# Turning softmax probabilities in one DVE instruction with a DMA block exchange, and reordered opening and seam work

## The reference

```python
xn = _layernorm(x); h = rmsnorm(xn) * ln_weight
h_q, h_k, h_v = h @ w_q.T, ctx @ w_k.T, ctx @ w_v.T       # (8, 128, 32 heads, 128)
score = einsum('bqhd,bkhd->bhqk', h_q, h_k) + position_bias
score = softmax(where(mask, score, -inf)); score = where(mask, score, 0)
out = einsum('bhqk,bkhd->bqhd', score, h_v).reshape(8, 128, 4096) @ w_out.T
x = x + tanh(g_xattn) * (xn + out)
x = x + tanh(g_ffn) * (base(x') + top-2 of 28 rank-8 experts(x')),  x' = _layernorm(x)
```

## Time and profile before

| | us |
|---|---|
| median of three runs | 888.44 (887.14 to 889.11) |
| the profiled execution | 888.88 |
| its span | 887.1 |
| PE busy in it | 867.6 |
| DVE / ACT / POOL busy | 655.4 / 359.6 / 308.5 |
| one iteration of the main loop | 40.47 |

### The profile page before, as it was taken

One profiled execution on the slowest core, in us unless ns is written; L12 is line 12 of the kernel. 1 busy time (PEld: TensorE's weight loads), 2 busy tenths in 40 slices (PEclk: granted clock), 3 DMA queues, 4 the chain that ended last, 5 costly groups with the idle time before them and its releaser, 6 DMA issues.

```text
span 887.1 us, 15278 instructions
## 1 busy us (share of the span) xinstructions
PE 867.6 (98%) x5128; PEld 768.2 (87%) x5128; DVE 655.4 (74%) x1295; ACT 359.6 (41%) x966; POOL 308.5 (35%) x218
## 2 busy tenths in 40 slices
PE   8989999998999999999999999999999999999998
PEld 7868888887998989898999989898989999898786
DVE  6885655659696877778696968778686969698863
ACT  5564444444253353434252443434252524444320
POOL 1476656686132332423142323323231423222200
PEclk9999999999999999999999999999999999999999
DMA  9124454454121221212121211203121202211001
GB/s 317 39 95 154 152 190 154 156 175 143 48 100 48 76 87 37 100 34 91 47 85 39 100 60 64 95 30 100 47 77 47 100 26 98 93 52 55 18 25 71
DMA packets 29074, 78.23 MB, mean 88 GB/s; under 512 B 4352, under 2 KB 6400, under 8 KB 27136
## 3 DMA queue, kind: packets, MB, share of 16 engines
q1 hardware_dynamic: 29056, 78.00, 25.6%
HBM read 60.16 MB, written 17.83 MB: 88 GB/s over the span
## 4 chain that ended last, share of the span: by engine, by line
PE 85%; DVE 8%; POOL 2%; issue 2%; DMA 1%; ACT 1%; SPq 0%; POOLq 0%; DVEq 0%; ACTq 0%
PE proj_ps L1112 53%; PE proj_ps L1285 13%; PE score_ps L1143 3%; PE score_ps L1171 3%; PE proj_ps L1463 2%; DVE attn L909 2%; PE pv_ps L1171 2%; PE turn_ps L1171 2%; PE proj_ps L1229 1%; PE pv_ps L1143 1%; PE turn_ps L1143 1%; PE proj_ps L1481 1%; DMA w_raw<-in_weights 1%; PE pv_ps L1112 1%; PE turn_ps L1112 1%
## 5 line engine op out<-in xcount | busy, mean ns | idle before, releaser
L347 POOL TENSOR_TENSOR w_lo<-w_raw,w_hi 128x1024 fp32r<-128x1024 f32 x49 | 118.4, 2417 | 360.9 <-ACT w_hi L444 287.0
L909 DVE STREAM_TRANSPOSE attn<-attn 32x256 f32<-32x256 f32 x480 | 209.1, 436 | 6.7
L1112 PE MATMUL proj_ps<-w_hi,ct_hi 128*128 128x256 f32 x512 | 146.2, 285 | 0.0
L1112 PE MATMUL proj_ps<-w_lo,ct_hi 128*128 128x256 f32 x512 | 144.8, 283 | 0.0
L1112 PE MATMUL proj_ps<-w_hi,ct_lo 128*128 128x256 f32 x512 | 144.8, 283 | 0.0
L925 DVE TENSOR_TENSOR acc<-proj_ps,acc 128x512 f32<-128x512 f32 x112 | 77.5, 692 | 66.7 <-PE proj_ps L1112 65.8
L464 ACT ACTIVATE attn<-attn,neg_max 128x128 f32<-128x128 f32 x256 | 99.2, 389 | 36.4 <-DVE neg_max L890 36.4
L444 ACT ACTIVATE w_hi<-w_raw 128x1024 fp32r<-128x1024 f32 x49 | 51.9, 1058 | 122.7 <-PE proj_ps L1112 118.8
L1112 PEld LDWEIGHTS proj_ps<-w_hi,ct_lo 128*128 128x128 f32 x512 | 98.2, 192 | 0.7
L1112 PEld LDWEIGHTS proj_ps<-w_hi,ct_hi 128*128 128x128 f32 x512 | 98.2, 192 | 0.7
L1112 PEld LDWEIGHTS proj_ps<-w_lo,ct_hi 128*128 128x128 f32 x512 | 98.1, 192 | 0.0
(11 more groups left out here) (199 smaller groups left out, 1777.6 us busy)
## 6 DMA issues: line engine op xcount, KB each, us to landing
w_raw<-in_weights SPq DMA_DIRECT2D x67, 512.0 KB, 3.3
q_spill<-attn SPq DMA_DIRECT2D x60, 256.0 KB, 3.0
qt<-q_spill SPq DMA_DIRECT2D x15, 1024.0 KB, 7.3
acc<-in_x SPq DMA_DIRECT2D x4, 512.0 KB, 8.9
bias_sb<-in_bias SPq DMA_DIRECT2D x16, 128.0 KB, 2.0
out<-attn SPq DMA_DIRECT2D x8, 256.0 KB, 2.0
w_raw<-in_x SPq DMA_DIRECT2D x6, 256.0 KB, 2.9
qt<-in_ctx_t SPq DMA_DIRECT2D x4, 256.0 KB, 5.4
```

The source lines that it names most:

```text
L347: pool.tensor_tensor(lo, w_raw[:, k, :], hi.bitcast(F32), ALU.subtract).then_inc(w_lo_done[k], 1)
L909: tr = dve.transpose(probs_t[k:k + Q32, t, :, :, q:q + Q32].rearrange("k j b q -> k (j b) q"), probs[q:q + Q32, HP * t:HP * t + HP, :, k:k ...
L1112: mm = pe.matmul(o, lhs(l, n), rhs(r, n), start=(start and n == 0 and m == 0), stop=(stop and n == terms - 1 and m == 2))
```

## The change

**The turn.** `turn_probs` becomes one DVE transpose over all 128 partitions and 1024 elements. It turns every 32x32 block where it is, into a new buffer `block_sb`, whose layout has the target group `a` of 32 partitions outermost. What remains is to move block (row group k, target a) to row group a. A new function `exchange(a, t)` on SP does that: one DMA stores the buffer (128 partitions of 4 KB, 512 KB) to DRAM, SP waits until it has landed, and four DMAs load 128 KB each into 32 partitions of `probs_t`, in rows of 1 KB. `probs_t` now holds for each key partition four groups of 32 queries, 1 KB apart, and `pv` reads its moving operand in four pieces of 32. `pv` waits on `block_in`. In the last phase the turn is PE's before and after; only its copy is written in the new layout.

**DVE's order.** `turn_probs(a, 0)` stands ahead of `add_bias(a, 3)`, and `turn_probs(a, 1)` right behind `normalise(a, 3)`. POOL's `add_mask(p)` moves behind the wait for all four normalised units.

**The opening.** POOL's first `s_forms` waits for the normalised x (`xn_done`). The remainder of the fourth block sum (T4) moves from POOL to DVE. `tf_hi` and `tf_lo` shrink to two forms (this makes room for `block_sb`); the two others lie in the v and k slots of `w_hi`/`w_lo` during the q loop, so the leads of the next k and v weights wait on ACT for the fourth and the last product of the last `q_phase`.

**The seam.** `mask_add` moves from POOL at the seam to DVE behind `q_phase(0)`. POOL then makes `comb` of phase 0 ahead of `rest(WK, 1)`, and the remainder of the weights kept for the experts (`w_lo[:, WQ]`) moves from the seam to behind the loop.

```diff
-        tf_hi, tf_lo = sb("tf_hi", [P, TF, 2, HALF], F32R), sb("tf_lo", [P, TF, 2, HALF], F32R)
+        tf_hi, tf_lo = sb("tf_hi", [P, 2, 2, HALF], F32R), sb("tf_lo", [P, 2, 2, HALF], F32R)
...
+        block_sb = sb("block_sb", [P, 2, HP * BU * S])
...
-        probs_t = attn[:, UNITS * BU * S:].rearrange("p (t j b s) -> p t j b s", t=2, j=HP, b=BU)
+        probs_t = attn[:, UNITS * BU * S:].rearrange("p (t a n q) -> p t a n q", t=2, a=NB, n=HP * BU)
+        blocks = [block_sb[:, t, :].rearrange("p (a n q) -> p a n q", a=NB, n=HP * BU) for t in range(2)]
+        block_spill = [nc.dram_tensor(f"block_spill{t}", (P, NB, HP * BU * Q32), F32, kind="Internal").ap() for t in range(2)]
...
+        def t_form_at(s, n):
+
+            if n < 2:
+                return (tf_hi, tf_lo)[s][:, n, :, :]
+            return (w_hi, w_lo)[s][:, (WV, WK)[n - 2], :].rearrange("p (c s) -> p c s", c=2)
...
+            def exchange(a, t):
+
+                sp.wait_ge(blocks_done, a * 2 + (t + 1))
+                sp.dma_start(block_spill[t], blocks[t].rearrange("p a n q -> p a (n q)")).then_inc(block_out[t], 16)
+                sp.wait_ge(block_out[t], a * 16 + 16)
+                for k in range(NB):
+                    rows = slice(k * Q32, (k + 1) * Q32)
+                    sp.dma_start(probs_t[rows, t, :, :, :].rearrange("p a n q -> p a (n q)"),
+                                 block_spill[t][:, k, :].rearrange("(a k) n -> k a n", k=Q32)).then_inc(block_in[t], 16)
...
                 load_q(p)
+                for t in range(2):
+                    exchange(p - 1, t)
                 load_bias(p + 1)
...
+            pool.wait_ge(xn_done, B)
             s_forms(0)
             rest_s(0, 0, 0)
-            pool.wait_ge(t_hi_done, 2)
-            pool.tensor_tensor(tf_lo[:, 3, :, :], t_raw[3], tf_hi[:, 3, :, :].bitcast(F32), ALU.subtract).then_inc(t_lo_pool, 1)
             rest_s(0, 1, 1)
...
-            rest(WK, 1)
-            pool.wait_ge(mask_in, 16)
-            pool.tensor_scalar(mask_add[:, :, :], mask_u8[:, :, :], 1.0, -NEG, ALU.subtract, ALU.mult).then_inc(mask_done, 1)
             pool.wait_ge(mask_done, 1)
             add_mask(0)
+            rest(WK, 1)
             rest(WV, 1)
             rest(WO, 0)
-            pool.wait_ge(w_hi_done[WQ], 2)
-            pool.tensor_tensor(w_lo[:, WQ, :], w_raw[:, WQ, :], w_hi[:, WQ, :].bitcast(F32), ALU.subtract).then_inc(w_lo_done[WQ], 1)
             with pool.Fori(1, LAST) as p:
+
+                pool.wait_ge(probs_done, (p - 1) * UNITS + UNITS)
                 add_mask(p)
-
-                pool.wait_ge(probs_done, (p - 1) * UNITS + UNITS)
...
                 if last:
+                    product(i, 4)
+                    lead(WK, 1)
+                    product(i, 7)
+                    lead(WV, 1)
                     return
...
+            rest_t(3, 2)
             t_form(2, b_block(1, 1), b_block(0, 1))
...
+            dve.tensor_scalar(mask_add[:, :, :], mask_u8[:, :, :], 1.0, -NEG, ALU.subtract, ALU.mult).then_inc(mask_done, 1)
             ordered(dve.tensor_reduce(row_any[:, :], mask_u8[:, :, :], AX.X, ALU.max))
...
                 dve.wait_ge(probs_done, a * UNITS + (HP * t + HP))
-                for q in range(0, S, Q32):
-                    for k in range(0, S, Q32):
-                        tr = dve.transpose(probs_t[k:k + Q32, t, :, :, q:q + Q32].rearrange("k j b q -> k (j b) q"),
-                                           probs[q:q + Q32, HP * t:HP * t + HP, :, k:k + Q32].rearrange("q j b k -> q (j b) k"))
-                tr.then_inc(turn_copied, 1)
+                dve.transpose(blocks[t].rearrange("p a n q -> p n a q"),
+                              probs[:, HP * t:HP * t + HP, :, :].rearrange("p j b (a k) -> p (j b) a k", a=NB)).then_inc(blocks_done, 1)
...
                 else:
-                    pe.wait_ge(turn_copied, a * 2 + (t + 1))
+                    pe.wait_ge(block_in[t], a * (16 * NB) + 16 * NB)
...
-                    mm = pe.matmul(pv_bank(a, u)[:, i * S:(i + 1) * S], v_sb[:, b, j * DH:(j + 1) * DH], probs_t[:, t, j, i, :],
+                    mm = pe.matmul(pv_bank(a, u)[:, i * S:(i + 1) * S], v_sb[:, b, j * DH:(j + 1) * DH], probs_t[:, t, :, j * BU + i, :],
                                    start=True, stop=True)
```

45 lines of the change are left out of this document (24 added, 21 removed).

## The result

| | before | changed |
|---|---|---|
| runs beside each other, median us | 887.79 (886.14 to 889.11) | 901.18 (898.95 to 903.37) |
| ratio, 95% interval | 1 | 1.0146 (1.012 to 1.0172) |
| profiled execution, span | 887.1 | 901.6 (time 903.37) |
| PE busy, share | 867.6, 98% | 871.0, 97% |
| DVE busy, share | 655.4, 74% | 486.7, 54% |

What follows compares the result with a forecast made beforehand. PE bounds the kernel, busy 867.6 of 887.1 us, and alone forms the loop's chain. Gains of 3.2 (opening), 4.1 (seam) and 1.1 (end) sum to 8.4, loop 0: 880.0 us, range 877.0 to 885.5 (forecast case 877.5 to 882).

Steps and rivals of the forecast that it cites:

- (a): Loop exchange: the 512 KB store to DRAM takes 3.4 us, ends 2.9 and 4.5.
- (d): Loop exchange: the last 128 KB load lands in 2.3 us, ends 2.0 and 3.1.
- The sentence on the ports: Loads into 32 partitions: 8 of 16 ports, about 218 GB/s, so the exchange would end some 0.5 us later.
- (b): Loop exchange: SP's wake-up after the store takes 0.2 us, ends 0.1 and 0.4.
- (c): Loop exchange: of four load issues on SP, the fourth starts 1.35 us after the first.
- Rival 1: Main loop: exchange late in every iteration, over 9.0 us; at 10 us 898, slower; chance 0.16.
- The seam: Ahead of the main loop: PE's wait shrinks from 3.7 to 1.5 us, slow stretch gone; gain 4.1, ends 0.5 and 5.6.
- Rival 2: Seam: full queues hold the exchange until after 215, clock falls again; gain 0.5 for 4.1, 883.6 us; chance 0.15.
- The opening: First 60 us: earlier x and T4's remainder off POOL bring PE forward; gain 3.2 us, ends 1.0 and 4.3.
- Rival 3: Opening: gives 1 us at most, as POOL's remainders meet DVE's block sums; 882.2 us; chance 0.12.
- The end: Last iteration: PE's wait for the turn and a slow first matmul group go; gain 1.1 us, ends 0 and 1.3.
- The pieces of 32: `pv` matmuls: reading the moving operand in four pieces costs 0; a tenth more would be 2.7 us.

## Why the prediction was wrong

- **The store, term (a): the step that failed.** I took 3.4 us, ends 2.9 and 4.5, on the ground that the q load "has passed when the store's data start", read from one microsecond, 452 to 453, of one iteration whose q load landed in 4.9. It was the exception: the same load took 6.5 to 8.1 us in 13 of the other 14 iterations of that execution, and even this one landed at 453.29, 1.3 us behind the time at which the store would start. The page of before shows the median in its DMA section:

```profile
qt<-q_spill SPq DMA_DIRECT2D x15, 1024.0 KB, 7.3
```

  Issued 3.66 us ahead, such a load ends 3.6 us behind the store's issue, and the store 1.25 us behind that: 4.9. In the changed kernel the q load takes 7.9 in the median and the loop's store 5.5 (4.6 to 5.9; 5.34 in the chain above).
- **The last load (d).** 3.05 for 2.3, within my ends, and the same 3.03 with the q load out of the way. So (d) was 0.75 short on its own. The sentence on the ports had 0.5 us of it (the sentence doesn't say how 0.5 follows from its 2.4 and 1.3), and I had left it out of the sum.
- **Wake-up and issues, (b) and (c).** 0.02 for 0.2, and 1.32 for 1.35. The sum is 5.34 + 0.02 + 1.32 + 3.05 = 9.75 us (with the gaps) for 7.25. It is above my sum of high ends, 9.35. With (d) as measured and (a) as I had it, the exchange would have taken about 7.8 us and been in time; the step that decides is (a).
- **Rival 1** described the result, with its point at 9.0 us and its sign. At 10 us, the mean that was measured, it gave 898. It counted 15 overruns where there were 13 of 1.08 us each, the seam's wait and none in the last iteration, and it left out the slow group behind each wait, 0.27. 0.16 was too little, since its argument against, 1.6 us left, stood on term (a).
- **The transpose.** 1.245 us for 1.25, in all 30. Right.
- **The seam.** Rival 2 held too: the store takes 5.86 us behind q and the refills, PE stands 4.4 us and then runs at 0.56, and the seam costs 0.7 where I had a gain of 4.1:

```profile
212.00:214.56 2.56, 0.00 (x0) 0.00 (x1) 0.00 (x0) 0.00 (x0) 2.56 (x2) 1.00 0.94 308
214.56:217.97 3.41, 3.41 (x17) 3.41 (x18) 0.69 (x1) 0.60 (x1) 0.96 (x1) 0.56 0.34 112
```

  The columns are stretch, us, busy of PE, PEld, DVE, ACT and POOL, clock, DMA, GB/s, as in the earlier trace rows. Without the q load ahead the wait is 2.3 where I had 1.5, and the exchange 8.2 where I had 7.25; most of that is the last load's 0.75.
- **The opening.** PE reaches its first half-size product at 57.94 in place of 60.25: 2.3, for 3.2 predicted. In the kernel with only the q load moved, which is the same up to there, it is 56.98, 3.3 less than before. So single executions differ by 1 us here, as much as the miss. Rival 3 (1 us at most) didn't come.

```profile
57.94 0.47 PE L1307 MATMUL proj_ps<-w_hi 128*128 128x512 f32 x1 [1.11 <-DVE attn L876]
```

- **The end.** 1.2 for 1.1. **The pieces of 32.** The groups of 8 take 0.89 us as in the earlier trace rows. **DVE's saved work.** 0, as predicted: the kernel with no exchange iterates in 40.47 us, as before. Right.
- **Without the failed step** the rest nearly stood: with the q load out of the way in the loop the kernel takes 882.3, inside the range of 877.0 to 885.5, but 2.3 above 880.0 and just outside 877.5 to 882. The loop iterates in 40.47 us there, as predicted; what is missing is at the seam.

## What to carry to other kernels

When a new transfer goes into a place where others already run, take the length of those others over all iterations, not from the window that one reads most closely: if the new one is issued before they are through, its landing time is theirs plus its own tail, here on either queue. A round trip that replaces engine work is worth its place only if everything that is issued just ahead of it can stand behind it; moving one 1 MB load from ahead to behind turned +1.5% into -0.7%. And ask of each in-order queue what the moved step now waits behind: that was wrong once in the prediction and more often in the expectations (the last q load, ACT's copy behind the exponentials, SP's store behind its refills, two rests of the last iteration).

## What the runs showed of the hardware

- A 512 KB store issued 0.9 to 3.7 us behind a 1 MB load ended 1.2 to 1.3 us behind that load's end in 39 loop iterations of three kernels, on the same queue or another; alone it took 2.6 us. Issued 0.55 us behind the last of four 128 KB loads it took 3.5 (second half of the changed kernel), and issued 1.4 behind it 2.6 (with only the q load moved).
- Four 128 KB loads into 32 partitions each landed 2.9 us after their issue in the median, into 128 partitions 2.4 (one execution each); the last of the four 3.0 and 2.5.
- SP issued 16 transfers between SBUF rows at 0.63 us each, 4 loads from DRAM at 0.44.
- One DVE transpose of 1024 elements on 128 partitions takes 1.245 us, where 16 of 256 elements on 32 take 7.17 together.
- PE's clock (mean of the 3.5 us behind a wait) stayed at 1.00 behind every loop wait of up to 1.54 us (changed kernel, 13 waits; with the q load on ACT behind the third unit up to 1.19). Behind waits of 1.45 to 1.91 us it fell in 3 of 13 (q load held back on SP), to 0.57 to 0.64; behind waits of 2.4 us in 11 of 13 (16 transfers without DRAM), to 0.52 to 0.66. Behind the seam's wait of 2.3 us it fell in one kernel (only the q load moved: 0.71 from 211.49 to 215) and not in another that is the same up to there (last q load moved too: 1.00). So the same wait costs about 1.6 us more in one execution or iteration than in the next.
